# A graph network on one core: a second set of four selector buffers while adjacency matrices are built, and selectors made ahead of the adds

## The chip, the cores and the metric

The kernel runs on one core of a Trainium2 chip. The metric is the time of one execution on the device in microseconds; less is better. The core has five engines, each with an instruction queue of its own: TensorE (PE in the profile, its weight loads PEld), VectorE (DVE), ScalarE (ACT), GpSimd (POOL) and SyncE (SP). They order themselves by semaphores. TensorE reads SBUF and writes PSUM; a granted clock of 1.0 is 2.4 GHz, of 0.5 1.2 GHz.

## What is computed

Four blocks over one graph of 6250 nodes with 128 features and 106250 edges, sorted by destination: three layers of a relational convolution (8 relations, weights mixed of 4 bases), one weighted mean aggregation, two further relational layers, one unweighted mean aggregation. Each block ends in a residual and a layer norm. Cut to what matters:

```python
def rel_graph_conv(h, src, dst, etype, coef, bases, loopw, bias):
    c, hs = coef[etype], h[src]
    m = sum(c[:, b:b + 1] * (hs @ bases[b]) for b in range(4))
    return segment_sum(m, dst, num_segments=h.shape[0]) + h @ loopw + bias

def mean_layer(x, src, dst, weight, W, b):       # weight is 1 in the second one
    agg = segment_sum(x[src] * weight, dst, n)
    deg = clip(segment_sum(weight, dst, n), 1.0)
    return concatenate([x, agg / deg]) @ W.T + b

# block 1: x = layernorm(x + R(R(R(x)))), each R = relu(rel_graph_conv(h)) + h
# block 2: x = layernorm(x + mean_layer(x, edge_weight))
# block 3: x = layernorm(x + R5(R4(x)))           # relu(agg + x @ SW + b)
# block 4: x = layernorm(x + mean_layer(x, 1))
```

The kernel counts seven layers: 0, 1, 2 relational, 3 mean (weighted), 4, 5 relational, 6 mean.

## The kernel before

**A relational layer** runs over 832 tiles of 128 edges, 16 tiles a turn, 52 turns, in halves of 8 tiles (h = 0 and 1), each half in two quarters q of 4 tiles. GpSimd gathers the source rows of each tile by an indirect transfer into a ring of 16 slots (L630); it begins a half's 8 gathers when TensorE has summed that half of the turn before (`summed`). In every fourth turn slot 15 is filled by SyncE instead, which fetches 128 single rows (`lent`). VectorE makes one-hots over 16 destinations by 8 relations for each tile (`onehots`, L1284). TensorE multiplies rows by one-hots (the "sum", L1056, two PSUM banks), ScalarE moves the sums to SBUF (L763), TensorE multiplies them by the weights of the 8 relations (the "message", L1067, `MSG[h]`), and VectorE adds the 8 tiles' 16 columns to the accumulator one after the other (`adds`, L1296), because neighbouring tiles overlap.

The destinations come in 13 chunks of 512 nodes. When the turns that reach a chunk are over (about every four turns), each engine does a chunk step between two turns: `columns` (L1503, L1507) on VectorE, transposes on TensorE (L1104, L910), copies on ScalarE, in layers 2 and 5 the layer norm too.

**Filling.** The mean layers use a dense adjacency matrix, 6272 by 6272, in device memory. It is built from the edge list while the relational layers run: the weighted one in layers 1 and 2, the other one, of marks in bf16, in layers 4 and 5. Each half turn makes four "fills" of two windows each. For a fill f, VectorE makes selectors in SBUF (`hots`: L1377 the low selector, 2 x 196 columns, and L1381 twice the weighted row selector, or L1386 once the row marks); TensorE multiplies the two (`fill`, L946, bank AGG); ScalarE copies the bank to a staging buffer (`keep_fill`, L733) and after every second fill stores it (L737). Layer 0 builds nothing.

**The order around the change.** TensorE in a half: sum of quarter 0, fill 0, sum of quarter 1, fill 1, four relations' messages, fill 2, the other four, fill 3. The fill waits for `hots_made` and for `fill_kept`, and everything behind it in the queue waits with it. VectorE in a turn i: selectors of half 0, one-hots of half 1, adds of half 0, selectors of half 1, one-hots of half 0 of turn i+1, adds of half 1. There are four pairs of buffers, one for each f. The selectors for fill f wait until the fill f of the half before is done, since `filled` starts at 4:

```python
for f in range(4):
    dve.wait_ge(filled, H * 4 + (f + 1))
```

The adds of half h wait for `messaged[h]`, TensorE's last message of that half. So in the queue of VectorE the selectors of a half stand behind the adds of the half in front.

`rel_w` (8192 bytes in each of 128 partitions) holds the weights of layers 4 and 5. It is loaded by ScalarE's queue near the start (L686). The region `scratch` holds the selector buffers and the staging buffers. SyncE's `lend_passes` fetches the single rows and, in layer 0, lays the edge table from which the matrices' lists are gathered (`table_part`).

`P` is the number of passes over the edges, `more` is P - 1; with this graph P is 1 and `more` 0, and `more_slices` is 0 too: the branches for them are passed by.

## Time and profile before

| | us |
|---|---|
| median of 3 runs | 7132.64 (7103.35 to 7148.3) |
| the profiled execution | 7121.17 |
| its span, first to last instruction | 7118.9 |
| PE busy | 5280.1 (74%) |
| DVE busy | 3967.8 (56%) |
| POOL busy | 3900.0 (55%) |
| ACT busy | 1620.4 (23%) |
| mean granted TensorE clock | 0.808 |

Busy shares are means over stages with different limits, so the stages are read one by one. A row of the timeline names start, duration, engine, line, operation, the tensors out<-in, how often, and in brackets the idle time of the engine before it and what ended it. "issue" is idle time in which the engine waited for nothing that the profile shows. The selector buffers, the gathered rows and the sums all lie in one tensor called `bulk`. A matmul of f32 operands shows as two instructions.

### The profile page before, as it was taken

The numbers are of one execution on the slowest core, as the hardware profiler recorded it, in microseconds if no ns is written. First come the engines' busy times: TensorE is split into PE (matmuls) and PEld (weight loads), VectorE is DVE, ScalarE is ACT, GpSimd is POOL, SyncE is SP. The second block draws the span as 40 slices with busy tenths as digits, with TensorE's granted clock in tenths as the row PEclk, the third lists the DMA queues.
The fourth block names the chain that finished last, engine by engine and source line by source line (L and its number), as shares of the span: only waits on it lengthen the run. The fifth ranks groups of instructions, "written<-read, shape, count | busy, mean of one in ns | idle before, by whom it ended". The sixth has DMA issues, their size and how long they took to land.

```text
span 7118.9 us, 132757 instructions
## 1 busy us (share of the span) xinstructions
PE 5280.1 (74%) x25722; PEld 4285.0 (60%) x25723; DVE 3967.8 (56%) x10739; ACT 1620.4 (23%) x3108; POOL 3900.0 (55%) x4125
## 2 busy tenths in 40 slices
PE   6766667777777777777899866666676676667998
PEld 4655666666666666666555466665656666655554
DVE  3222226666666666666666555555545555556665
ACT  1111113322323222222100122222232222221000
POOL 6777776666666666666200066666656666662000
PEclk8777778988989889888899967767666666677998
DMA  3222224444444444444688544444434444445886
GB/s 97 63 67 67 70 69 115 125 124 121 128 123 115 120 114 123 117 117 116 198 285 279 192 118 121 123 120 125 121 110 117 114 119 114 113 117 192 277 284 201
DMA packets 719129, 966.83 MB, mean 136 GB/s; under 512 B 103155, under 2 KB 601199, under 8 KB 718543
## 3 DMA queue, kind: packets, MB, share of 16 engines
q0 software_dynamic: 131872, 271.19, 16.1%
q10 hardware_dynamic: 481717, 354.21, 15.9%
q1 hardware_dynamic: 105210, 338.21, 14.2%
q14 instruction: 267, 2.19, 0.1%
q8 instruction: 63, 1.03, 0.1%
HBM read 608.12 MB, written 361.06 MB: 136 GB/s over the span
## 4 chain that ended last, share of the span: by engine, by line
PE 52%; issue 15%; DVE 13%; POOL 9%; DVEq 6%; ACT 2%; DMA 1%; ACTq 0%; POOLq 0%; SPq 0%
PE msg L1067 17%; PE agg L946 10%; POOL bulk L630 9%; PE sum L1056 8%; DVE acc L1296 8%; PE sum L972 8%; PE msg L972 6%; DVEq L1296 2%; ACT bulk L763 2%; DVE bulk L1381 1%; DVE bulk L1386 1%; PE lin L920 1%; DMA bulk<-in_x_dram,srcT_i 1%; DVEq L159 1%; DVEq L1377 1%
## 5 line engine op out<-in xcount | busy, mean ns | idle before, releaser
L630 POOL DMA_INDIRECT bulk<-h_table,srcT_i x3276 | 3107.7, 949 | 2272.3 <-issue 927.8
L946 PE MATMUL agg<-bulk 128*128 128x196 f32 (+1 forms) x4992 | 1228.2, 364 | 1129.4 <-DVE bulk L1386 572.0
L1296 DVE TENSOR_TENSOR acc<-msg,acc 128x16 f32 x4160 | 728.9, 175 | 2307.5 <-PE msg L1067 1811.4
L1056 PE MATMUL sum<-bulk 128*128 128x128 f32 x8320 | 1539.2, 337 | 345.4 <-DMA bulk<-in_x_dram,srcT_i 210.0
L1056 PEld LDWEIGHTS sum<-bulk 128*128 128x128 f32 x8320 | 1383.2, 244 | 463.9 <-issue 251.2
L946 PEld LDWEIGHTS agg<-bulk 128*128 128x128 f32 (+1 forms) x4992 | 812.7, 188 | 1243.5 <-issue 1201.6
L733 ACT ACTIVATE bulk<-agg 128x392 f32<-128x392 f32 x1664 | 826.5, 497 | 2462.1 <-PE agg L946 2411.2
L1377 DVE TENSOR_TENSOR bulk<-iota_ps,low_key 128x392 f32<-128x392 f32 (+1 forms) x1664 | 927.9, 558 | 277.1 <-issue 277.1
L763 ACT ACTIVATE bulk<-sum 128x512 f32<-128x512 f32 x1040 | 621.1, 597 | 1680.3 <-PE sum L1056 1602.7
L630 POOL DMA_INDIRECT bulk<-in_x_dram,srcT_i x819 | 777.5, 949 | 279.5 <-issue 257.8
L1067 PE MATMUL msg<-bulk,mix_w 128*128 128x128 f32 x4992 | 834.3, 326 | 112.2 <-ACT bulk L763 101.2
L1067 PE MATMUL msg<-bulk,rel_w 128*128 128x128 f32 x3328 | 808.5, 422 | 123.4 <-ACT bulk L763 123.4
L1067 PEld LDWEIGHTS msg<-bulk,mix_w 128*128 128x128 f32 x4992 | 775.5, 236 | 185.3 <-issue 176.8
L1067 PEld LDWEIGHTS msg<-bulk,rel_w 128*128 128x128 f32 x3328 | 728.7, 322 | 196.6 <-issue 193.7
L1411 DVE TENSOR_TENSOR bulk<-bulk 128x1792 f32<-128x1792 f32 (+1 forms) x384 | 688.2, 1792 | 223.3 <-DMA bulk<-adjacency_w 97.4
L1284 DVE TENSOR_TENSOR bulk<-iota_ps,keyT 128x512 f32<-128x512 f32 x1040 | 665.0, 680 | 59.9 <-issue 45.0
L972 PE MATMUL sum<-bulk,hT 128*128 128x448 f32 x1568 | 660.8, 552 | 30.9 <-issue 13.4
L1381 DVE TENSOR_SCALAR bulk<-iota_ps,row_key,weight_of 128x128 f32<-128x128 f32 x1664 | 598.2, 400 | 0.0
L972 PEld LDWEIGHTS sum<-bulk,hT 128*128 128x128 f32 x1568 | 299.4, 194 | 329.1 <-issue 328.8
L972 PE MATMUL msg<-bulk,hT 128*128 128x448 f32 x1176 | 494.9, 544 | 0.0
L972 PEld LDWEIGHTS msg<-bulk,hT 128*128 128x128 f32 x1176 | 225.8, 192 | 222.1 <-issue 222.1
L1386 DVE TENSOR_TENSOR bulk<-iota_ps,row_key 128x256 bf16<-128x256 f32 x832 | 344.5, 414 | 0.0
(170 smaller groups left out, 1014.9 us busy)
## 6 DMA issues: line engine op xcount, KB each, us to landing
adjacency_w<-bulk ACTq DMA_DIRECT2D x416, 392.0 KB
adjacency_n<-bulk ACTq DMA_DIRECT2D x416, 392.0 KB
bulk<-adjacency_w SPq DMA_DIRECT2D x147, 896.0 KB, 4.6
bulk<-adjacency_n SPq DMA_DIRECT2D x147, 896.0 KB, 5.0
lent<-h_table SPq DMA_DIRECT2D x6656, 0.5 KB
bulk<-h_table,srcT_i POOLq DMA_INDIRECT x3276
lent<-in_x_dram SPq DMA_DIRECT2D x1664, 0.5 KB
bulk<-adjacency_w SPq DMA_DIRECT2D x49, 448.0 KB, 4.2
```

Source lines behind the costliest of these rows:

```text
L630: nc.gpsimd.indirect_dma_start(out=rows_in[:, s, :], out_offset=None, in_=rows_of[:, :], in_offset=bass.IndirectOffsetOnAxis(ap=srcT_i[:, ...
L733: act.activation(staged[s][:, f % 2 * 2 * LOWS:(f % 2 + 1) * 2 * LOWS], AGG[:, 0:2 * LOWS], ACT.Copy).then_inc(fill_kept, 1)
L763: act.activation(sums[:, h, :, 4 * (q % 2):4 * (q % 2) + 4, :].rearrange("p r t v -> p t r v"), SUM[q % 2][:, :].rearrange("p (t r v) -> p ...
L946: last = nc.tensor.matmul(AGG[:, w * LOWS:(w + 1) * LOWS], row[:, w, :], of[:, w, :], start=True, stop=True)
L972: last = nc.tensor.matmul(DENSE[s][:, 0:PIECE], x_rows[:, n, :], a_in[t % A_BUFS][:, s * PIECE:(s + 1) * PIECE], start=(n == 0), stop=(n = ...
L1056: last = nc.tensor.matmul(SUM[q % 2][:, t * KEYS:(t + 1) * KEYS], rows_in[:, 4 * q + t, :], onehot[:, 4 * q + t, :], start=True, stop=True)
L1067: last = nc.tensor.matmul(MSG[h][:, 0:HALF * WIN], W[:, n, :], sums[:, h, n, :, :].rearrange("p t v -> p (t v)"), start=(n == 0), stop=(n ...
L1284: nc.vector.tensor_tensor(onehot[:, 4 * q:4 * q + 4, :], IOTA[:, 0:KEYS].unsqueeze(1).broadcast_to(each), keyT[:, bass.ds(i * RING + 4 * q ...
L1296: nc.vector.tensor_tensor(acc[:, at], MSG[h][:, s * WIN:(s + 1) * WIN], acc[:, at], ALU.add).then_inc(added, 1)
L1377: nc.vector.tensor_tensor(low_hots[f] if weighted else low_marks[f], IOTA[:, KEYS:NATURAL].unsqueeze(1).broadcast_to(each), low_key[:, bas ...
L1381: ins = nc.vector.tensor_scalar(row_hots[f][:, n, :], IOTA[:, NATURAL:NATURAL + D], row_key[:, bass.ds(w + n, 1)], weight_of[:, bass.ds(w ...
L1411: nc.vector.tensor_tensor(a_sum[:, 0:wide], a_in[t % A_BUFS][:, 0:wide], a_sum[:, 0:wide], ALU.add).then_inc(a_counted, 1)
```

## The change

- VectorE's order in a building turn i is now: one-hots of half 1, selectors of half 1, adds of half 0, one-hots of half 0 of turn i+1, selectors of that half, adds of half 1. The selectors of the layer's very first half are made ahead of the loop.
- There are eight pairs of buffers: four for half 0, four for half 1. The second four low selectors and one row selector lie in `rel_w`'s memory, three row selectors behind the staging buffers in `scratch`. For the marks (bf16), which need half the bytes, the second set lies in the other half of the first four buffers and `rel_w` isn't touched.
- `filled` starts at 8 instead of 4, and the selectors for fill f wait for the fill f of two halves ago.
- `rel_w` is loaded at the head of layer 3 instead of near the start; TensorE waits for it in layers 4 and 5.
- The table of edges is laid in the last pass of layer 0 alone, where it was laid in every pass; with P = 1 that is the same work. A call outside of the loop takes the place of the loop's one round.

The diff, cut to its core:

```diff
-        low_hots = [scratch[:, f * 2 * LOWS:(f + 1) * 2 * LOWS].rearrange("p (w n) -> p w n", w=2) for f in range(4)]
-        row_hots = [scratch[:, 8 * LOWS + f * 2 * D:8 * LOWS + (f + 1) * 2 * D].rearrange("p (w n) -> p w n", w=2) for f in range(4)]
+        rel_w = sb("rel_w", [D, 2, N_RELS, D])
+        spare = rel_w[:, :, :, :].rearrange("p n r d -> p (n r d)")
+        kept_from = 8 * LOWS + 8 * D + 8 * LOWS
...
+        low_hots = pairs(scratch, 0, LOWS, 4) + pairs(spare, 0, LOWS, 4)
+        row_hots = pairs(scratch, 8 * LOWS, D, 4) + pairs(spare, 8 * LOWS, D, 1) + pairs(scratch, kept_from, D, 3)
...
-                with sp.Fori(0, P) as p:
+                def lend_pass(p, laying):
                     K = sp.snap(P * (REL_BEFORE[l] * QUADS) + p * QUADS)
                     for n in range(QUADS):
                         fetch(l, n, sp.snap(K + n))
                         place(n, sp.snap(K + n))
-                        if l == 0:
+                        if laying:
                             table_part(n)
...
+                with sp.If(more > 0):
+                    with sp.Fori(0, more) as p:
+                        lend_pass(p, False)
+                lend_pass(more, True)
...
-            act.dma_start(rel_w[:, :, :, :], rel_ws).then_inc(late_weights_in, 16)
...
-                act.wait_ge(filled, H * 4 + (f + 5))
+                act.wait_ge(filled, H * 4 + (f + 9))
...
                     if m == 0:
+                        act.dma_start(rel_w[:, :, :, :], rel_ws).then_inc(late_weights_in, 16)
...
-            pe.sem_inc(filled, 4)
+            pe.sem_inc(filled, 8)
...
                 for w in range(2):
-                    row, of = (row_hots[f], low_hots[f]) if weighted else (row_marks[f], low_marks[f])
+                    b = h * 4 + f
+                    row, of = (row_hots[b], low_hots[b]) if weighted else (row_marks[b], low_marks[b])
...
                         W = rel_w[:, layer["lin"] - 3, :, :]
+                        pe.wait_ge(late_weights_in, 48)
...
                     for f in range(4):
-                        dve.wait_ge(filled, H * 4 + (f + 1))
+                        dve.wait_ge(filled, H * 4 + (f + (5 if h is None else 1)))
...
                     def opened(p):
 
                         onehots(0, 0, dve.snap(count(P, p, r, 0)))
+                        if layer["fills"] and p is more:
+                            fill_at(0, 0)
                         dve.wait_ge(acc_set, 2 + CHUNKS * (r + 1))
 
                     def turn(i, k, filling=False):
-                        if filling:
-                            fill_at(i, 0)
                         onehots(1, i, k)
-                        adds(0, i, k)
                         if filling:
                             fill_at(i, 1)
+                        adds(0, i, k)
                         with dve.If(i < TURNS - 1):
-                            onehots(0, nc.s_assert_within(i + 1, min_val=1, max_val=TURNS - 1,
-                                                          skip_runtime_bounds_check_because="the condition above"), k + 1)
+                            following = nc.s_assert_within(i + 1, min_val=1, max_val=TURNS - 1,
+                                                           skip_runtime_bounds_check_because="the condition above")
+                            onehots(0, following, k + 1)
+                            if filling:
+                                fill_at(following, 0)
                         adds(1, i, k)
```

## Rows read from the trace of the kernel before

**Rows 1.** Busy time by stage: stretch, length, engines' busy (instructions), clock, DMA share, GB/s
```profile
core 0: us, PE busy (x) PEld busy (x) DVE busy (x) ACT busy (x) POOL busy (x), PEclk, DMA share, GB/s
200.00:1060.00 860.00, 594.67 (x2880) 514.66 (x2881) 243.51 (x894) 115.58 (x195) 650.45 (x685) 0.73 0.26 68
1086.00:2234.00 1148.00, 826.74 (x4994) 763.14 (x4993) 747.57 (x2269) 345.00 (x651) 777.12 (x819) 0.89 0.45 122
2262.00:3435.00 1173.00, 848.38 (x4999) 778.47 (x4997) 773.61 (x2407) 344.65 (x652) 775.61 (x818) 0.87 0.43 117
3460.00:4081.00 621.00, 589.61 (x1776) 311.43 (x1774) 403.99 (x427) 40.96 (x99) 0.00 (x0) 0.97 0.77 260
4083.00:5241.00 1158.00, 788.63 (x4157) 701.66 (x4155) 607.85 (x1848) 334.45 (x647) 774.64 (x819) 0.71 0.43 121
5271.00:6464.00 1193.00, 819.19 (x4184) 728.79 (x4182) 634.63 (x1972) 333.36 (x653) 776.05 (x818) 0.68 0.41 115
```

**Rows 2.** Waits, whole span: who waited for whom, us in total, times, longest
```profile
POOL bulk L630 <- PE sum L1056: 663.0, 306, 14.1
PE agg L946 <- DVE bulk L1386: 572.0, 208, 5.2
PE agg L946 <- DVE bulk L1381: 557.1, 207, 5.6
PE sum L1056 <- DMA bulk<-in_x_dram,srcT_i: 210.0, 313, 1.8
```

**Rows 3.** Timeline of TensorE in layer 1, one half turn
```profile
2025.54 0.90 PE L946 MATMUL agg<-bulk 128*128 128x196 f32 x4 [2.68 <-DVE bulk L1381]
...
2035.66 0.90 PE L946 MATMUL agg<-bulk 128*128 128x196 f32 x4 [2.77 <-DVE bulk L1381]
```

**Rows 4.** Timeline of VectorE in layer 1, the same stretch
```profile
2024.05 0.57 DVE L1377 TENSOR_TENSOR bulk<-iota_ps,low_key 128x392 f32<-128x392 f32 x1 [0.18 <-issue]
2024.53 0.72 DVE L1381 TENSOR_SCALAR bulk<-iota_ps,row_key,weight_of 128x128 f32<-128x128 f32 x2
...
2028.50 1.28 DVE L1284 TENSOR_TENSOR bulk<-iota_ps,keyT 128x512 f32<-128x512 f32 x2
2031.18 2.34 DVE L1296 TENSOR_TENSOR acc<-msg,acc 128x16 f32 x8 [1.41 <-PE msg L1067]
2034.16 0.57 DVE L1377 TENSOR_TENSOR bulk<-iota_ps,low_key 128x392 f32<-128x392 f32 x1 [0.64 <-issue]
```

**Rows 5.** Timeline of GpSimd in layer 1, the same stretch
```profile
2018.41 0.95 POOL L630 DMA_INDIRECT bulk<-h_table,srcT_i  x1 [2.02 <-PE sum L1056]
...
2024.67 0.95 POOL L630 DMA_INDIRECT bulk<-h_table,srcT_i  x1 [0.31 <-issue]
```

**Rows 6.** Timeline around a chunk step in layer 2, VectorE and TensorE
```profile
2857.27 0.60 PE L1104 MATMUL lin<-ident,y 128*128 128x128 f32 x4
2859.71 0.69 DVE L1503 SCALAR_TENSOR_TENSOR y<-acc,hT 128x512 f32 x1 [0.49 <-DVE acc L1296]
2863.04 2.07 PE L1056 MATMUL sum<-bulk 128*128 128x128 f32 x8 [4.21 <-issue]
2865.09 0.57 DVE L1377 TENSOR_TENSOR bulk<-iota_ps,low_key 128x392 f32<-128x392 f32 x1 [1.05 <-issue]
```

**Rows 7.** Timeline of TensorE in layer 4, a half at the lower clock
```profile
4605.74 1.11 PE L1056 MATMUL sum<-bulk 128*128 128x128 f32 x8
...
4614.73 1.94 PE L1056 MATMUL sum<-bulk 128*128 128x128 f32 x8
...
4621.75 1.08 PE L1056 MATMUL sum<-bulk 128*128 128x128 f32 x8
```

**Rows 8.** Timeline in layer 0: a gather and the sum that reads it
```profile
861.61 0.95 POOL L630 DMA_INDIRECT bulk<-in_x_dram,srcT_i  x1 [0.30 <-issue]
...
864.30 0.79 PE L1056 MATMUL sum<-bulk 128*128 128x128 f32 x2 [0.83 <-DMA bulk<-in_x_dram,srcT_i]
```

**Rows 9.** Timeline at the end of layer 1: last fill, next layer's first gather
```profile
2252.40 0.90 PE L946 MATMUL agg<-bulk 128*128 128x196 f32 x4
...
2262.00 0.95 POOL L630 DMA_INDIRECT bulk<-h_table,srcT_i  x1 [27.14 <-DMA h_table<-rows]
```

More of the change, by code:

```diff
@@ L244, in build, with pairs @@
         landed_i = scratch.bitcast(I32).rearrange("p (g t e) -> p g t e", t=3, e=D)
-        low_hots = [scratch[:, f * 2 * LOWS:(f + 1) * 2 * LOWS].rearrange("p (w n) -> p w n", w=2) for f in range(4)]
-        row_hots = [scratch[:, 8 * LOWS + f * 2 * D:8 * LOWS + (f + 1) * 2 * D].rearrange("p (w n) -> p w n", w=2) for f in range(4)]
-        low_marks, row_marks = ([hot.rearrange("p w n -> p (w n)").bitcast(BF16)[:, 0:2 * n].rearrange("p (w n) -> p w n", w=2) for hot in hots]
+        rel_w = sb("rel_w", [D, 2, N_RELS, D])
+        spare = rel_w[:, :, :, :].rearrange("p n r d -> p (n r d)")
+        kept_from = 8 * LOWS + 8 * D + 8 * LOWS
+        def pairs(at, first, n, many):
+            return [at[:, first + f * 2 * n:first + (f + 1) * 2 * n].rearrange("p (w n) -> p w n", w=2) for f in range(many)]
+        low_hots = pairs(scratch, 0, LOWS, 4) + pairs(spare, 0, LOWS, 4)
+        row_hots = pairs(scratch, 8 * LOWS, D, 4) + pairs(spare, 8 * LOWS, D, 1) + pairs(scratch, kept_from, D, 3)
+        low_marks, row_marks = ([hots[f].rearrange("p w n -> p (w n)").bitcast(BF16)[:, h * 2 * n:(h + 1) * 2 * n]
+                                 .rearrange("p (w n) -> p w n", w=2) for h in range(2) for f in range(4)]
                                 for hots, n in ((low_hots, LOWS), (row_hots, D)))
@@ L305, in build @@
         basis = sb("basis", [D, 3, N_BASES, D])
-        rel_w = sb("rel_w", [D, 2, N_RELS, D])
         mix_w = sb("mix_w", [D, N_RELS, D])
@@ L500, in lend_passes @@
                         place(n, sp.snap(K + n))
-                        if l == 0:
+                        if laying:
                             table_part(n)
+                if l:
+                    with sp.Fori(0, P) as p:
+                        lend_pass(p, False)
+                    return
+                more = sp.value_load(passes[0:1, 1:2], min_val=0, max_val=MAX_PASSES - 1)
+                with sp.If(more > 0):
+                    with sp.Fori(0, more) as p:
+                        lend_pass(p, False)
+                lend_pass(more, True)
             def load_adjacency(matrix, B, pass_of):
@@ L589, in gather_again @@
                     apart(pool)
-                pool.wait_ge(filled, pool.snap(built * FILLS + 4))
+                pool.wait_ge(filled, pool.snap(built * FILLS + 8))
                 apart(pool)
@@ L641, in _ @@
                     pool.wait_ge(at_set, 1)
-                    pool.wait_ge(edges_out, pool.snap(P * (16 * (3 * QUADS - WEIGHTS_FROM)) + 32))
-                    apart(pool)
+                    pool.wait_ge(edges_out, 16 * (3 * QUADS - WEIGHTS_FROM) + 32)
                     gather_lists()
@@ L936, in turn_lists, with fill @@
                 apart(pe)
-            def fill(H, f, weighted):
+            def fill(H, f, weighted, h=0):
                 pe.wait_ge(hots_made, H * 4 + (f + 1))
@@ L1038, in between @@
                         def between(h, f):
-                            fill(first + h, f, m == 0)
+                            fill(first + h, f, m == 0, h)
                         messages(i, k, between)
@@ L1262, in _ @@
                 if l == 1:
-                    dve.wait_ge(late_weights_in, 48)
+                    dve.wait_ge(late_weights_in, 32)
                     for n in range(2):
@@ L1368, in key_lists, with hots @@
                                             window_key[:, :].unsqueeze(2).broadcast_to([D, LANES, D]), ALU.subtract).then_inc(keys_ready, 1)
-                def hots(H, at, weighted):
+                def hots(H, at, weighted, h=None):
                     for f in range(4):
-                        dve.wait_ge(filled, H * 4 + (f + 1))
+                        dve.wait_ge(filled, H * 4 + (f + (5 if h is None else 1)))
                         apart(dve)
-                        w = at * 8 + 2 * f
+                        w, f = at * 8 + 2 * f, (h or 0) * 4 + f
                         each = [D, 2, LOWS]
@@ L1438, in fill_at @@
                         at = dve.snap(i * 2 + (part_of * 2 * TURNS + h))
-                        hots(dve.snap(at + (more_slices + 1) * HALVES) if of else at, at, of == 0)
+                        hots(dve.snap(at + (more_slices + 1) * HALVES) if of else at, at, of == 0, h)
                     def opened(p):
                         onehots(0, 0, dve.snap(count(P, p, r, 0)))
+                        if layer["fills"] and p is more:
+                            fill_at(0, 0)
                         dve.wait_ge(acc_set, 2 + CHUNKS * (r + 1))
                     def turn(i, k, filling=False):
-                        if filling:
-                            fill_at(i, 0)
                         onehots(1, i, k)
-                        adds(0, i, k)
                         if filling:
                             fill_at(i, 1)
+                        adds(0, i, k)
                         with dve.If(i < TURNS - 1):
-                            onehots(0, nc.s_assert_within(i + 1, min_val=1, max_val=TURNS - 1,
-                                                          skip_runtime_bounds_check_because="the condition above"), k + 1)
+                            following = nc.s_assert_within(i + 1, min_val=1, max_val=TURNS - 1,
[3 more added lines that the diff above has]
+                                fill_at(following, 0)
                         adds(1, i, k)
```

## The prediction, made before the change was run

> **What bounds the kernel now.** I read the busy times by stage first, with one stretch for each relational layer from its first gather to its last [rows 1]. Layer 0, which builds no matrix, issued 685 gathers in 860 us, 1.256 us for each; at that pace the 819 gathers of a layer take 1028 us. Layers 1, 2, 4 and 5, which build, took 1148, 1173, 1158 and 1193 us. They exceed the gathers' pace by 120, 145, 130 and 165 us, 560 us together. Everything the change can give lies in these four stretches and at their ends.
>
> The waits over the whole span come next [rows 2]: TensorE stood 557.1 us for the weighted selectors of layers 1 and 2 and 572.0 us for the marks of layers 4 and 5, each time at `fill`. GpSimd in its turn stood 663.0 us for a `sum` of TensorE, so it is not its own pace that holds it there. The wait for a gather, 210.0 us, belongs to layer 0 alone.
>
> The third view is one half turn on each engine. TensorE [rows 3]: the fill at 2025.54 and the fill at 2035.66 are the first ones of two halves, 10.12 us apart, and 2.77 us of this is idle until VectorE has made a selector. TensorE's own work in the half is 7.35 us. VectorE [rows 4]: selectors from 2024.05, one-hots from 2028.50, then 1.41 us idle until the messages of the half are there, the adds at 2031.18, and only behind them, at 2034.16, the selectors of the next half. This is the loop: messages, adds, selectors, fill, messages. The selectors cannot be made ahead, because they stand behind the adds in the queue and because their four buffers are those that TensorE is just reading. GpSimd [rows 5]: a gather is 0.95 us and the issue before it 0.30, but the first of a half waited 2.02 us for the sum that frees its slots. The loop sets the pace and GpSimd follows.
>
> **The change, part by part.** *Order and buffers.* The adds of a half now stand behind the selectors of the next one, which have buffers of their own. When TensorE reaches a fill, its selectors were made about one half earlier. The 557.1 + 572.0 = 1129 us of waiting leave TensorE. The gain is smaller, because another pace ends last then. Three candidates:
>
> GpSimd: 16, 16, 16 and 15 gathers in four turns are 15.75 a turn, by 1.256 us 19.8 us.
>
> VectorE: from the selectors at 2024.05 to those at 2034.16 are 10.11 us, less the wait of 1.41 us 8.70 us [rows 4]. This half has the 0.64 us of issue at the loop's end; with 0.18 in its place, as at 2024.05, the other half is 8.24 us, together 16.9 us. To this comes the chunk step: from 2859.71 to the selectors at 2865.09 are 5.4 us in layer 2 [rows 6], 12 or 13 times in 52 turns, 1.3 us a turn. About 18.2 us, 1.6 us under GpSimd. The marks are cheaper than the weighted selectors, so layers 4 and 5 have more room.
>
> TensorE: the layers' stretches less the waits at the fills are (1148 + 1173 - 557) / 104 = 17.0 us a turn for layers 1 and 2, and (1158 + 1193 - 572) / 104 = 17.1 for 4 and 5, chunk steps in it. That is 2.7 us under GpSimd. It holds for the clocks granted now, 0.89, 0.87, 0.71 and 0.68 [rows 1]. In layer 4 at 1.2 GHz (matmul groups of 1.94 us instead of 1.11) the stretch from one `sum` to that of the next half is 7.0 us [rows 7], with that one's own 1.94 us and a fill some 9.2, 18.4 us a turn and with the chunk steps (from 2857.27 to 2863.04, 5.8 us [rows 6], every fourth turn) 19.8: no more than GpSimd needs even if the higher level is never granted.
>
> So the four layers fall back on the gathers' pace, as layer 0 does. Bounds for what remains: none, or the whole of the present chunk steps' delay. In layer 2 such a step costs TensorE 4.21 us of idle and a first group at the lower clock, 2.07 us where 1.11 is usual [rows 6, 7], and 12 steps of 5 us are 60 us. Against that stands the room of the ring: with 16 slots, GpSimd gathers one half (10.0 us) while TensorE has the other to sum. A sum stands 2.7 us behind its gather in layer 0, from 861.61 to 864.30 [rows 8], so TensorE may be some 7 us late before GpSimd has to stand. One step fits, a step plus a slow half does not quite. I take 20 us a layer (1 us for each step, and a few for the first turn), 80 us together. Gain in the four stretches: 560 - 80 = 480 us.
>
> *The ends of the layers.* In layer 1 the last gather ended 27.14 us before the next layer's first one at 2262.00, at 2234.86, and the last fill started at 2252.40 [rows 9]: TensorE was still working through a backlog. At the gathers' pace there is none: 2.7 us from issue to sum and about 5 us for messages and fills, 8 us instead of 18. The tail behind it stays. 10 us by four layers are 40 us; bounds 0 and 44.
>
> *`rel_w` lends four buffers,* so its load of 1024 KB moves from the start to the head of layer 3 on ScalarE's queue. Nothing of ScalarE waits behind it but one issue. At the 260 GB/s that the DMA engines move in this stage [rows 1] it is 4 us of traffic in a stage in which TensorE is busy 589.61 of 621 us; between 0 and 4 us, I take 2. The wait for it in layer 4 stands 600 us later and costs nothing. At the start the traffic is saved; what is loaded there before the first gathers is not waited for, 0.
>
> *The rest* costs nothing: with one pass, SyncE's lending loop issues the same transfers behind one more branch, and it is ahead of TensorE; the table's rows are laid in the same places; the semaphore counts that start at 8 are the same instructions; the marks of the second set lie in the other half of the same floats. The selectors of the first half of a layer are made once ahead of the loop, 4.5 us of VectorE, in place of those in the first turn. The branch that now stands between the adds and the one-hots was covered by queued selectors before; if nothing covers it, it is a few tenths of a us a turn on VectorE, which has 1.6 to give.
>
> *A rule to weigh.* The gather that began at 2024.67 took its usual 0.95 us although VectorE's selectors filled the whole stretch around it, those with the scalar form from 2024.53 and again later [rows 4, 5]. So selectors and gathers pass each other without a price. The Trainium skill (SBUF — State Buffer, "Who interferes with whom") says that `tensor_scalar` can run in a mode that holds the port pair shared with GpSimd and blocks descriptor writing. By that rule this change, which packs VectorE tighter, would be paid in gathers; by the row it isn't, the trace disagrees with so broad a reading, and the page itself limits the mode to operands in SBUF, while the iota read here lies in PSUM.
>
> **Sum.** The profiled span of 7118.9 us - 480 - 40 + 2 = 6601 us. The run lasted 7121.17, 2 us more, and the median of the runs shown, 7132.64, lies 11 us above that: 6601 + 14 = 6615 us.
>
> **Rivals.**
> VectorE doesn't get ahead. It is one queue in order, and the adds still wait for messages. If it kept standing 1.41 us a half [rows 4], its turn would be 18.2 + 2.8 = 21.0 us, 52 turns 1092 us instead of 1048, four layers 176 us more: 6790 us. For it: 18.2 of 19.8 us leaves little, and after a chunk step it is late by about 4 us and wins back only 0.8 a half. Against it: TensorE is then waiting for gathers, so the wait at the adds is room and not loss. 0.13.
>
> TensorE's clock. Layer 0, which waits for gathers, was granted 0.73, layers 1 and 2 now 0.89 and 0.87 [rows 1]. If their level fell to 0.65, 17.0 us would be 17 x 0.88 / 0.65 = 23 us a turn, 1196 us a layer, nothing won in layers 1 and 2: 6615 + 2 x 148 = 6910 us. Against it: TensorE stands 24% of these layers now and would stand 14%. The Trainium skill (TensorE: Matmul & The Clock Gate, "Part 1: The HAM clock gate") has the lower level as the default that activity lifts; that speaks the same way. 0.06.
>
> The wait only moves. If TensorE stood at the fills as long as before, for instance because the selectors wait for buffers of `filled` counted wrongly late, nothing changes: 7130 us. Against it: the new count asks for the fill of two halves ago, which is behind the messages that the adds in front already waited for. 0.04.
>
> Slower. If GpSimd's gathers stood while VectorE runs the scalar-form selectors, eight pairs of 0.72 us a turn [rows 4] would be 5.8 us added to 19.8. Two weighted layers would lose 600 us against the 520 won: 7210 us or a little over. It decides from 5 us a turn on. The gather at 2024.67 is against it. 0.03.
>
> **How the numbers follow.** The forecast has 0.74, its own range 6550 to 6710 (no rest of the 80 us and 4 more at the ends below; twice the rest above). The range of 8 in 10 takes in the VectorE case: 6550 to 6800. A measurement of this kernel tells about 1% from no change. Faster by over 1%: forecast, VectorE and clock cases, 0.93. Within 1%: 0.04. Slower: 0.03.
>
> **What would show it.** The waits of TensorE for VectorE at `fill` gone (under 50 of 1129 us), waits for gathers in their place; the wait of GpSimd for `sum` under 80 us instead of 663.0; each of the four stretches within 1028 to 1065 us; the granted clock in layers 4 and 5 the same or higher; VectorE's wait for messages in the building layers still there and above 0.5 us a half; the fill after the last gather of layer 1 some 8 us behind it. The prediction is wrong if TensorE's time a turn without waits passes 19.8 us, if VectorE has no wait for messages left, or if the gathers' pace leaves 1.25 us.

## The result, and the profile after

The changed kernel takes 6482.93 us (median of four runs, 6481.08 to 6490.13), against 7140.47 us for the kernel before (four runs, 7103.35 to 7152.13). The ratio is 0.909 [0.906, 0.912]. The forecast of 6615 us had the direction and the mechanism, but the gain is larger than its range allowed: 6483 lies below the 6550 at which it began. The profiled execution took 6490.13 us with a span of 6488.0 us, 630.9 less than before; the forecast had taken 518 off the span.

The four layers that build, with the mean layer 3 between them, each from its first gather to its last. This is the table of busy times by stretch of the kernel after, with the granted clock (PEclk) and the share and rate of the DMA engines:

```profile
core 0: us, PE busy (x) PEld busy (x) DVE busy (x) ACT busy (x) POOL busy (x), PEclk, DMA share, GB/s
1083.60:2111.20 1027.60, 827.50 (x5021) 736.80 (x5020) 754.06 (x2292) 336.21 (x653) 775.52 (x819) 0.94 0.50 137
2128.60:3152.90 1024.30, 840.94 (x5017) 747.17 (x5016) 778.23 (x2433) 337.61 (x654) 774.84 (x819) 0.93 0.49 135
3184.00:3766.00 582.00, 574.74 (x1690) 300.48 (x1689) 382.17 (x355) 26.36 (x63) 0.00 (x0) 0.98 0.79 268
3794.70:4816.70 1022.00, 733.75 (x4184) 619.63 (x4183) 612.35 (x1862) 326.28 (x652) 772.51 (x818) 0.81 0.50 138
4833.40:5855.90 1022.50, 733.71 (x4204) 622.53 (x4202) 639.74 (x1994) 325.19 (x656) 773.12 (x818) 0.80 0.49 135
```

Set beside [rows 1], the stretches of layers 1, 2, 4 and 5 went from 1148, 1173, 1158 and 1193 us to 1027.6, 1024.3, 1022.0 and 1022.5. They are now all alike, and 819 gathers in 1022 us are 1.248 us each: the gathers' own pace and next to nothing beside it. TensorE's clock rose in all four, in layers 4 and 5 most, from 0.71 and 0.68 to 0.81 and 0.80.

The waits over the whole span (engine and line waited for, us in total, times, the longest):

```profile
DVE acc L1315 <- PE msg L1086: 1240.1, 394, 8.3
PE sum L1075 <- DMA bulk<-h_table,srcT_i: 642.2, 625, 3.1
POOL bulk L648 <- PE sum L1075: 53.7, 124, 12.5
```

The 557.1 and 572.0 us in which TensorE stood for VectorE at `fill` [rows 2] have no line left. At the sums of the building layers TensorE now waits for gathers, 642.2 us, where the kernel before has no such wait (its 210.0 us are those of layer 0, and 211.5 after). GpSimd's wait for a sum fell from 663.0 to 53.7 us, and 20.9 of these lie in layer 0. TensorE stands as much as the gathers leave it.

GpSimd, TensorE and VectorE in one turn of layer 1 (start, us, engine, line, tile; in brackets the idle time before and what ended it):

```profile
1995.10 0.94 POOL L648 DMA_INDIRECT bulk<-h_table,srcT_i  x1 [0.30 <-issue]
...
2005.08 0.94 POOL L648 DMA_INDIRECT bulk<-h_table,srcT_i  x1 [0.30 <-issue]
```

```profile
1997.61 0.48 PE L1075 MATMUL sum<-bulk 128*128 128x128 f32 x2 [1.96 <-DMA bulk<-h_table,srcT_i]
1997.98 1.26 PE L964 MATMUL agg<-rel_w,bulk 128*128 128x196 f32 x4
```

```profile
1995.08 1.29 DVE L1303 TENSOR_TENSOR bulk<-iota_ps,keyT 128x512 f32<-128x512 f32 x2
1996.29 0.56 DVE L1396 TENSOR_TENSOR bulk<-iota_ps,low_key 128x392 f32<-128x392 f32 x1
...
2003.26 2.33 DVE L1315 TENSOR_TENSOR acc<-msg,acc 128x16 f32 x8 [2.45 <-PE msg L1086]
...
2007.40 0.56 DVE L1396 TENSOR_TENSOR rel_w<-iota_ps,low_key 128x392 f32<-128x392 f32 x1
```

Before, a fill stood 2.77 us for a selector behind the adds [rows 3, 4]. Now selectors start at 1996.29 behind the one-hots, the adds of the half in front come at 2003.26, 2.45 us idle until their messages are there, and the fill at 1997.98 runs without waiting. The idle time is VectorE's. GpSimd's gathers follow each other every 1.25 us. And the views of GpSimd and TensorE show how much room the ring has. The fills around 1998 read `rel_w`, so the sum that ends at 1997.61 + 0.48 = 1998.09 is the last one of a half 1. Counted from the layer's first gather (16 a turn, 15 in every fourth), that is turn 45, the gather at 1995.10 opens half 0 of turn 46, and eight gathers later, at 2005.08, GpSimd asks for the slots of half 1 again. TensorE was 7.0 us ahead of that. The same difference for all halves of this layer, from the times at which the trace has the semaphore `summed` counted up, has a median of 7.6 us and never passes 8.2. Call this the margin; the experiments below act on it.

The end of layer 1, where [rows 9] showed a backlog: the last gather, the last fill and the next layer's first gather.

```profile
2111.19 0.94 POOL L648 DMA_INDIRECT bulk<-h_table,srcT_i  x1 [0.30 <-issue]
...
2128.55 1.03 POOL L648 DMA_INDIRECT bulk<-h_table,srcT_i  x1 [16.42 <-DMA h_table<-rows]
```

```profile
2118.94 0.90 PE L964 MATMUL agg<-rel_w,bulk 128*128 128x196 f32 x4
```

The last fill starts 6.8 us behind the last gather's end (2112.13) where it was 17.5, and GpSimd stands 16.42 us instead of 27.14.

### The profile page after: what moved, and what is told of

Read it like the earlier page. It is cut to its first block, busy times and chain, and to the rows that moved or that the text cites. A ratio compares the mean times of both kernels' runs of the same rounds, so it can differ in the third digit from the quotient of the medians.

```text
span 6488.0 us, 133021 instructions
## 1 busy us (share of the span) xinstructions
PE 5095.0 (79%) x25722; PEld 4005.7 (62%) x25723; DVE 3958.4 (61%) x10739; ACT 1581.1 (24%) x3108; POOL 3890.0 (60%) x4125
## 3 DMA queue, kind: packets, MB, share of 16 engines
q0 software_dynamic: 131872, 271.19, 18.2%
## 4 chain that ended last, share of the span: by engine, by line
POOL 49%; PE 22%; issue 22%; DMA 5%; DVE 1%; ACTq 1%; ACT 1%; POOLq 0%; DVEq 0%; SPq 0%
POOL bulk L648 49%; PE sum L990 8%; PE msg L990 7%; DMA bulk<-h_table,srcT_i 4%; PE sum L1075 2%; PE msg L1086 1%; PE agg L964 1%; DMA bulk<-in_x_dram,srcT_i 1%; PE iota_ps L1114 1%; PE lin L937 1%; PE lin L1115 0%; DMA bulk<-adjacency_w 0%; DMA bulk<-adjacency_n 0%; ACTq L688 0%; PE lin L1007 0%
## 5 line engine op out<-in xcount | busy, mean ns | idle before, releaser
L1075 PE MATMUL sum<-bulk 128*128 128x128 f32 x8320 | 1576.1, 318 | 1015.5 <-DMA bulk<-h_table,srcT_i 642.2
L1075 PEld LDWEIGHTS sum<-bulk 128*128 128x128 f32 x8320 | 1253.8, 212 | 1300.2 <-DMA bulk<-h_table,srcT_i 636.9
L1315 DVE TENSOR_TENSOR acc<-msg,acc 128x16 f32 x4160 | 728.2, 175 | 1746.8 <-PE msg L1086 1240.1
L1086 PE MATMUL msg<-bulk,mix_w 128*128 128x128 f32 x4992 | 856.4, 332 | 104.5 <-ACT bulk L779 90.7
L1086 PEld LDWEIGHTS msg<-bulk,mix_w 128*128 128x128 f32 x4992 | 796.8, 242 | 175.5 <-issue 168.0
L1086 PE MATMUL msg<-bulk,rel_w 128*128 128x128 f32 x3328 | 686.1, 372 | 120.8 <-ACT bulk L779 120.3
L964 PE MATMUL agg<-bulk 128*128 128x196 f32 (+1 forms) x3328 | 726.3, 326 | 20.6 <-ACT bulk L749 20.0
L1086 PEld LDWEIGHTS msg<-bulk,rel_w 128*128 128x128 f32 x3328 | 613.7, 276 | 179.5 <-issue 177.0
L1396 DVE TENSOR_TENSOR bulk<-iota_ps,low_key 128x392 bf16<-128x392 f32 (+1 forms) x1248 | 693.7, 556 | 0.0
L1400 DVE TENSOR_SCALAR bulk<-iota_ps,row_key,weight_of 128x128 f32<-128x128 f32 x1456 | 524.6, 402 | 0.0
L964 PEld LDWEIGHTS agg<-bulk 128*128 128x128 f32 (+1 forms) x3328 | 462.8, 161 | 67.7 <-issue 30.2
```

Of the source, the lines that this page charges most:

```text
L964: last = nc.tensor.matmul(AGG[:, w * LOWS:(w + 1) * LOWS], row[:, w, :], of[:, w, :], start=True, stop=True)
L1075: last = nc.tensor.matmul(SUM[q % 2][:, t * KEYS:(t + 1) * KEYS], rows_in[:, 4 * q + t, :], onehot[:, 4 * q + t, :], start=True, stop=True)
L1086: last = nc.tensor.matmul(MSG[h][:, 0:HALF * WIN], W[:, n, :], sums[:, h, n, :, :].rearrange("p t v -> p (t v)"), start=(n == 0), stop=(n ...
L1315: nc.vector.tensor_tensor(acc[:, at], MSG[h][:, s * WIN:(s + 1) * WIN], acc[:, at], ALU.add).then_inc(added, 1)
L1396: nc.vector.tensor_tensor(low_hots[f] if weighted else low_marks[f], IOTA[:, KEYS:NATURAL].unsqueeze(1).broadcast_to(each), low_key[:, bas ...
L1400: ins = nc.vector.tensor_scalar(row_hots[f][:, n, :], IOTA[:, NATURAL:NATURAL + D], row_key[:, bass.ds(w + n, 1)], weight_of[:, bass.ds(w ...
```

## Experiments

The theory going in: the order of VectorE's work, with buffers to allow it, broke the loop of messages, adds, selectors and fill; what binds now is the issue of the gathers; the chunk steps, to which the forecast gave 20 us a layer, are absorbed by the ring's margin.

### Which half of the change does it

*The buffers alone.* The changed kernel, with VectorE's loop put back:

```diff
                         onehots(0, 0, dve.snap(count(P, p, r, 0)))
-                        if layer["fills"] and p is more:
-                            fill_at(0, 0)
...
                     def turn(i, k, filling=False):
+                        if filling:
+                            fill_at(i, 0)
                         onehots(1, i, k)
+                        adds(0, i, k)
                         if filling:
                             fill_at(i, 1)
-                        adds(0, i, k)
                         with dve.If(i < TURNS - 1):
...
-                            onehots(0, following, k + 1)
-                            if filling:
-                                fill_at(following, 0)
...
                         adds(1, i, k)
```

> The changed kernel with VectorE's order put back: selectors of a half behind the adds of the half in front, but eight pairs of buffers. Theory (the order is what counts): the selectors stand behind the adds in the queue as before, so TensorE waits at the fills as before, about 1100 us in all, and the time is that of the kernel before, 7140 us within 1%. Rival (the buffers were what held VectorE back): 6480 to 6550 us.

Measured: 7125.06 us in ten runs (7108.92 to 7158.43), ratio 0.9992 [0.9979, 1.0006]. Its waits:

```profile
POOL bulk L648 <- PE sum L1075: 700.3, 314, 11.9
PE agg L964 <- DVE bulk L1405: 556.2, 208, 5.4
PE agg L964 <- DVE bulk L1400: 284.7, 103, 5.6
PE agg L964 <- DVE rel_w L1400: 269.6, 104, 3.0
```

The picture of [rows 2]: 556.2 for the marks, 284.7 + 269.6 = 554.3 for the weighted selectors in the two sets. Eight buffers alone give nothing, as its theory expected.

*The order alone.* The kernel before with four selector buffers, `rel_w` loaded at the start and the counts untouched; only VectorE's loop is the new one (the same lines, the other way round, and `fill_at(0, 0)` in `opened`).

> The kernel before with the new order of VectorE and nothing else: four pairs of buffers, the selectors for fill f wait for the fill f of the half in front, the weights of layers 4 and 5 are loaded at the start. Theory A (the order is enough): fills 0 to 2 free their buffers before the messages end, only the fourth pair of selectors (1.1 us) is made behind the last fill; VectorE keeps 8.7 us of work in the 10.0 us of a half, TensorE finds its first selectors ready, and the time is 6480 to 6530 us. Theory B (order and buffers are both needed): the adds now stand behind the fourth selectors, which wait for the last fill, and the loop of one half in front of the other closes again through TensorE; 6800 us or more.

Measured: 6487.7 us (6482.54 to 6498.28), ratio 0.9102 [0.9082, 0.9122], the whole gain. Its waits, and VectorE in a turn of layer 1:

```profile
DVE acc L1296 <- PE msg L1067: 579.6, 107, 8.9
DVE bulk L1377 <- PE agg L946: 566.0, 599, 2.2
POOL bulk L630 <- PE sum L1056: 52.2, 116, 13.4
```

```profile
2000.49 0.57 DVE L1377 TENSOR_TENSOR bulk<-iota_ps,low_key 128x392 f32<-128x392 f32 x1
2002.16 0.57 DVE L1377 TENSOR_TENSOR bulk<-iota_ps,low_key 128x392 f32<-128x392 f32 x1 [0.46 <-PE agg L946]
2003.37 2.32 DVE L1296 TENSOR_TENSOR acc<-msg,acc 128x16 f32 x8
2006.30 1.29 DVE L1284 TENSOR_TENSOR bulk<-iota_ps,keyT 128x512 f32<-128x512 f32 x2 [0.60 <-issue]
```

With four buffers VectorE has to wait for the fill that frees each one (566.0 us in 599 short waits). But when it comes to the adds their messages are there, for the messages come between the same fills: 566.0 + 579.6 = 1145.6 us, about the 1240.1 us that it stands at the adds with eight. The time is spent once, ahead of the selectors or behind them, and it was idle in either case. The prediction's sentence that the selectors can't be made ahead "because their four buffers are those that TensorE is just reading" was wrong as a bar: TensorE releases them one by one, early enough.

### What binds now

*One gather less.* A gather into slot 7 is left out in every turn of every relational layer, and slot 6 is read twice in its place:

```diff
-                                if s == RING - 1 and i % QUAD == QUAD - 1:
+                                if s == 7 or s == RING - 1 and i % QUAD == QUAD - 1:
...
+                                    slot = 6 if 4 * q + t == 7 else 4 * q + t
```

> The changed kernel without the gather of slot 7; TensorE reads slot 6 twice, so one tile of 16 has wrong rows, and the work of all other engines is the same. Theory (the gathers' issue on GpSimd sets the pace in all five relational layers): 52 gathers of 1.25 us less in each layer, 65 us a layer, 325 us in all, 6155 us. Rival (another engine is as near the bound): VectorE's estimated 18.2 us a turn in layers 1 and 2 against 18.4 us of the gathers' pace would just not show, but if its true need is 19 us or more, layers 1 and 2 give at most 35 us each and the time is 6215 us or more.

Measured: 6169.06 us (6168.78 to 6169.35), ratio 0.8651 [0.863, 0.8673]. Layers 1 and 4 of the stretches:

```profile
1020.80:1986.20 965.40, 795.93 (x5026) 718.48 (x5026) 748.84 (x2287) 334.81 (x653) 727.60 (x767) 0.95 0.50 142
3601.40:4558.60 957.20, 707.68 (x4191) 598.93 (x4190) 608.18 (x1861) 327.03 (x652) 723.66 (x767) 0.81 0.50 143
```

Of the 819 gathers 52 are gone, by 1.25 us 65 us; the stretches shrank by 62.2 and 64.8 us. Layer 0 loses its 52 gathers too; five such layers are the 314 us between 6482.9 and 6169.1, where 325 were expected. TensorE and VectorE execute what they did. So the gathers' issue alone binds in all four building layers, the heavier 1 and 2 as well.

### Why the chunk steps cost nothing

The forecast's residual of 80 us was for these steps. One in layer 2 after the change, on TensorE, with the next gather into the slots that its sums free:

```profile
2472.12 0.60 PE L1123 MATMUL lin<-ident,y 128*128 128x128 f32 x4
...
2477.61 2.07 PE L1075 MATMUL sum<-bulk 128*128 128x128 f32 x8 [3.93 <-issue]
...
2480.78 1.91 PE L1075 MATMUL sum<-bulk 128*128 128x128 f32 x8
```

```profile
2484.50 0.95 POOL L648 DMA_INDIRECT bulk<-h_table,srcT_i  x1 [0.30 <-issue]
```

The step is as long as in [rows 6]: 3.93 us idle, then a group of 2.07 us where 1.15 is usual. The half's last sum ends at 2480.78 + 1.91 = 2482.69, the gather starts at 2484.50. Of a margin of some 7 us 1.81 are left, and the gather doesn't wait. GpSimd's waits for a sum inside the stretches of layers 1, 2, 4 and 5, in this order:

```profile
POOL bulk L648 <- PE sum L1075: 10.6, 26, 3.0
POOL bulk L648 <- PE sum L1075: 7.0, 23, 0.3
POOL bulk L648 <- PE sum L1075: 6.4, 21, 0.3
POOL bulk L648 <- PE sum L1075: 8.8, 29, 0.3
```

All but one of these are 0.3 us, which passes between any two gathers. The one of 3.0 us lies in the first turns of layer 1, where no step is yet. So late sums cost the gathers of the four layers 2.7 us together, and the steps nothing. To find where the margin ends, the steps were made longer: in the building layers their four transposes are repeated.

```diff
-                    for s in range(blocks_of(c)):
+                    for s in list(range(blocks_of(c))) * (5 if layer['fills'] else 1):
```

Five times:

> The changed kernel with the transposes of each chunk step in the layers that build done five times over on TensorE, 16 transposes more, 2.2 us at 2.4 GHz and up to twice that at 1.2 GHz. Theory (TensorE's lateness at a step is taken up by the ring of 16 slots, margin some 7 us, so the steps cost nothing within the turns): only the steps behind the last turn of a layer cost, about 3 us by four layers, 6495 us, and GpSimd's wait for sums grows by less than 30 us. Rival, the term of the prediction (a step costs a share of its length, and a longer one more): 48 steps by 2.2 us, 105 us more, 6590 us or above.

Measured: 6482.1 us (6480.41 to 6492.67), ratio 0.909 [0.9072, 0.9107], nothing lost. The same place:

```profile
2472.10 2.35 PE L1123 MATMUL lin<-ident,y 128*128 128x128 f32 x20
2478.07 1.15 PE L1075 MATMUL sum<-bulk 128*128 128x128 f32 x8 [3.19 <-issue]
2479.72 1.05 PE L1075 MATMUL sum<-bulk 128*128 128x128 f32 x8
```

This run didn't do what it was made for. The transposes take 1.75 us longer, but the idle time behind them shrank and the sums ran at the higher clock, 1.15 us instead of 2.07. The half's last sum ended at 2480.77, 8.67 us after the transposes began, where it was 10.57 us in the changed kernel: 1.9 us less. It is not this step alone. Of the eleven steps between the turns of layer 2, nine had the group behind the idle time at 2.07 us before, and three have it in this run. GpSimd's wait for sums stayed at 51.6 us. It shows that these longer steps are free, but it puts no load on the margin.

Twenty-five times:

> The changed kernel with the transposes of each chunk step in the building layers done 25 times over: 96 transposes more, 13 us at 2.4 GHz, of which some 4 us can lie in the idle time that the step has anyway. Theory (the ring's margin, some 7 us, of which the usual step takes up to 5.6 us): now each step makes GpSimd wait, about 13 - 4 - 2 = 7 us or more of 48 steps, 340 us and up, plus some 60 us behind the last turns: 6800 to 7000 us, and GpSimd's wait for sums is over 300 us instead of 53.7. Rival (TensorE has so much room that steps of any such length vanish over the next turns): below 6600 us.

Measured: 6745.45 us (6731.59 to 6759.32), ratio 0.9452 [0.9381, 0.9524].

```profile
2520.04 11.08 PE L1123 MATMUL lin<-ident,y 128*128 128x128 f32 x100
...
2534.88 1.41 PE L1075 MATMUL sum<-bulk 128*128 128x128 f32 x8 [3.32 <-issue]
...
2537.38 1.85 PE L1075 MATMUL sum<-bulk 128*128 128x128 f32 x8
```

```profile
2540.04 0.94 POOL L648 DMA_INDIRECT bulk<-h_table,srcT_i  x1 [7.86 <-PE sum L1075]
```

```profile
POOL bulk L648 <- PE sum L1075: 247.8, 181, 12.8
```

Now GpSimd stands 7.86 us for the sum, and the gather comes 0.81 us after it ended (2537.38 + 1.85 = 2539.23). Ten us more on TensorE (11.08 instead of 0.60) cost 2.6, 6.0, 2.4 and 5.3 us a step in layers 1, 2, 4 and 5: their stretches are 1056.5, 1090.1, 1048.6 and 1081.0 us, 28.9, 65.8, 26.6 and 58.5 more, and the trace has eleven steps within each. That is 180 of the 241.5 us of span; the rest, 62 us, lies outside these stretches, where some 60 were expected. So the price is there, and it starts only when the margin is gone. Inside the stretches it was less than expected (180 us for 340, and 247.8 us of waiting where over 300 was expected). The kind was right; what was wrong was to take the step of layer 2 for all. In the changed kernel the margin behind a step has a median of 6.8 and 7.1 us in layers 1 and 4, by the same reckoning as above, and of 2.8 and 3.0 us in layers 2 and 5, where the step holds the layer norm: the layers whose steps leave little are those in which the longer step costs twice as much. Since 0.81 us pass between sum and gather even where GpSimd waits, of the 1.81 us in the unchanged step shown about 1.0 is true room, and that step has to be so much later before it costs anything.

### Is the second set worth anything once gathers bind less

The guess: eight buffers pay where VectorE is the bound. With three gathers left out in every turn (slots 3, 7 and 11; slots 2, 6 and 10 are read twice) the gathers' pace is 12.75 × 1.249 = 15.9 us a turn, under what VectorE takes.

> The changed kernel without the gathers of slots 3, 7 and 11, TensorE reading the slots in front twice: three tiles of 16 have wrong rows, all other work is the same. The gathers' pace is 12.75 x 1.25 = 15.9 us a turn. Theory (next to the gathers stands VectorE with 18.2 us a turn in the weighted layers 1 and 2, and TensorE and VectorE with 16 to 17 us in layers 4 and 5): layer 0 falls by 195 us, layers 1 and 2 by 75 to 90 us each, layers 4 and 5 by 140 to 180 us each, and GpSimd waits for sums in layers 1 and 2. Rival (the gathers bound everything still): 975 us less, 5510 us.

Eight buffers, measured: 5749.16 us (5745.55 to 5752.77), ratio 0.8056 [0.8008, 0.8104]. The same with the order alone and four buffers:

> The kernel of e2_order_only (new order, four pairs of buffers) without the gathers of slots 3, 7 and 11; three tiles of 16 have wrong rows as in e6_three_gathers_less. There, with eight pairs, layers 1 and 2 took 897 and 921 us and VectorE hardly waited; 5749 us. Theory (the second set counts where VectorE is the bound): with four pairs VectorE's fourth selectors wait for TensorE's last fill, so the two engines take turns in part; layers 1 and 2 take 940 us or more each, layers 4 and 5 870 or more, and the time is 5850 us or above. Rival (the second set is worth nothing here either): within 20 us of 5749 us.

That run was on another chip, where it took 8090.36 us and the kernel before 9199.64: ratio 0.8793 [0.8767, 0.8818], and nothing can be said of the pair. So the two were run again side by side.

> The kernel of e7_three_less_four_buffers (new order, four pairs of buffers, gathers of slots 3, 7 and 11 left out) again, next to its twin with eight pairs on the same chip, because in e7 the kernel before took 9200 us where it took 7140 us elsewhere, so that e7 and e6 can't be compared. Theory (the second set counts where VectorE is the bound): at least 100 us above the twin. Rival: within 20 us of it.

> The kernel of e6_three_gathers_less (new order, eight pairs of buffers, gathers of slots 3, 7 and 11 left out) again, as the twin of e8_four_buffers_again: 5749 us if the kernel before takes 7140 us on this chip, and at least 100 us less than the twin by the theory, the same within 20 us by the rival.

Again a chip of that kind: 7989.29 us with four, 7895.69 with eight, and 8996.09 for the kernel before; ratios 0.8881 [0.8855, 0.8906] and 0.8777 [0.8751, 0.8802]. There, with three gathers fewer, the second set is worth 94 us (two runs of each), but in another regime. The wait rows of the run with eight, and one copy of ScalarE beside its fill on TensorE:

```profile
POOL bulk L648 <- PE sum L1076: 2116.4, 378, 15.4
ACT bulk L749 <- remote: 1977.8, 373, 8.0
```

```profile
1610.07 0.90 PE L964 MATMUL agg<-rel_w,bulk 128*128 128x196 f32 x4
```

```profile
1614.11 0.50 ACT L749 ACTIVATE bulk<-agg 128x392 f32<-128x392 f32 x1 [4.18 <-remote]
```

The fill is over at 1610.97, and ScalarE goes on to its copy 3.1 us later, by a releaser that the view can't name. The trace has the semaphore `filled`, for which the copy waits, counted up at 1614.00, 3.0 us behind the fill's end; in the same kernel on the chip with 7140 us this is 0.01 us. The other thing that the copy waits for, the store that frees its staging buffer, can't be it: it had landed by 1608.01. GpSimd waits 2116.4 us for sums. So in this trace a signal between engines comes late; why is open. The change itself, with all its gathers, wasn't run on such a chip. All four were then run on one chip, with the kernel before at 7140.66 us.

> The changed kernel itself, as the twin of e11_order_only_again. On a chip on which the kernel before takes 7140 us: 6483 us, the same as the twin within 10 us. On a chip of the kind with 9000 us: the theory (there engines wake late from waits and the gathers do not bind any more) expects the twin with four pairs of buffers 50 to 150 us slower.

> The kernel of e2_order_only again (new order, four pairs of buffers, all gathers). 6488 us, the same as e10_changed_again, where the gathers bind; 50 to 150 us above e10 on a chip of the kind with 9000 us.

> The kernel of e8_four_buffers_again (new order, four pairs of buffers, gathers of slots 3, 7 and 11 left out) on this chip. By the theory (the second set counts where VectorE is the bound) 100 us or more above its twin e13, by the rival within 20 us.

> The kernel of e6_three_gathers_less (new order, eight pairs of buffers, gathers of slots 3, 7 and 11 left out) on this chip: 5749 us where the kernel before takes 7140 us; by the theory 100 us or more under its twin e12.

| kernel | four buffers | eight buffers |
|---|---|---|
| all gathers | 6490.73 (6487.83 to 6493.63), 0.9089 [0.9062, 0.9115] | 6494.05 (6487.75 to 6500.35), 0.9093 [0.9067, 0.912] |
| three fewer a turn | 5757.64 (5754.56 to 5760.73), 0.8062 [0.8039, 0.8085] | 5747.95 (5745.44 to 5750.46), 0.8048 [0.8025, 0.8072] |

The guess fell, on this kind of chip. Layers 1 and 4 with four buffers, then layers 1, 2 and 4 with eight:

```profile
939.30:1838.10 898.80, 749.74 (x4985) 671.03 (x4986) 736.02 (x2261) 339.27 (x646) 628.23 (x663) 0.98 0.53 144
...
3434.10:4263.90 829.80, 626.87 (x4167) 533.40 (x4165) 608.36 (x1853) 327.45 (x650) 624.87 (x663) 0.89 0.57 157
```

```profile
931.90:1830.30 898.40, 748.33 (x4985) 669.00 (x4986) 735.82 (x2261) 340.03 (x646) 630.39 (x663) 0.98 0.53 144
1855.10:2774.60 919.50, 776.53 (x4999) 691.72 (x4997) 764.98 (x2407) 341.88 (x652) 627.26 (x663) 0.96 0.51 139
3418.30:4250.30 832.00, 630.06 (x4172) 540.35 (x4171) 604.07 (x1856) 327.50 (x651) 626.84 (x663) 0.88 0.57 156
```

Layer 4 is still at its gathers' pace (663 × 1.25 = 829 us). Layers 1 and 2 are not; 898.4 and 919.5 us are 17.3 and 17.7 us a turn, and with eight buffers VectorE has no wait for messages in layer 1. There it is VectorE's own turn that is seen, and it has the same length with four buffers (898.8). In layer 1 with four, TensorE's waits at the fills and VectorE's for a buffer:

```profile
PE agg L946 <- DVE bulk L1382: 63.1, 84, 0.8
DVE bulk L1378 <- PE agg L946: 0.7, 2, 0.5
```

TensorE stands for selectors, and VectorE stands 0.7 us in all for a buffer: four are released as fast as VectorE fills them. With three gathers fewer the two kernels differ by 10 us, with two runs of each, their ratios' intervals overlap, and the 100 us that were looked for are not there. Layers 1 and 2 fell by 129 and 105 us, where 75 to 90 were expected for e6: VectorE needs less for a turn than the 18.2 us of the prediction.

## Why the prediction was right, and where it was short

- *What bounds, and what would.* Right. The stretches exceeded the gathers' pace by all that the loop cost and fell back on that pace. The run with one gather less confirms it.
- *The turns of the engines.* GpSimd 19.8 us: measured 1022 to 1028 us over 52 turns, 19.7. VectorE 18.2: 17.3 and 17.7 in the runs where it binds, so the estimate was 0.5 to 0.9 us high, and the room under GpSimd is 2 us or more rather than 1.6.
- *The residual of 20 us a layer* is the step that failed, and it carries most of the miss. The text itself put about 7 us of ring room beside a step of 5 us, and the room was right: 7.0 us in the turn shown, 7.2 to 7.6 in the median of each layer. Then came "one step fits, a step plus a slow half does not quite", and each step was charged 1 us and each layer a few more. Here it went wrong. A step with its slow half does fit: no step in the four layers left less than 1.5 us, and late sums cost the gathers 2.7 us in all, ahead of the first step. 80 us forecast, 2.7 measured. The other bound, none, stood in the text and was the right one.
- *The gathers' pace.* 1.256 us came from a stretch of layer 0 divided by its gathers. From one gather to the next it is 1.253 us in the mean in the trace of before and 1.250 in that of after (the median gather 0.947 and 0.944 us); the rest are a few longer gathers and waits in that stretch. The four stretches come out at 1.248 to 1.255. By 819 gathers and four layers this is 16 us. With the residual it makes 96: the stretches gave 4672 - 4096.4 = 575.6 us, not 480.
- *The ends of the layers.* The span lost 630.9 - 575.6 = 55 us outside the four stretches, and not 40 - 2. From the start of the last gather to the end of the last add the four ends took 21.2, 25.3, 24.3 and 26.9 us before and 10.4, 13.4, 10.4 and 11.0 after, 52.4 us less together, 10.8 to 15.9 each where 10 was forecast (in layer 1 the last fill stands 6.8 us behind the last gather, 8 forecast). The upper bound of 44 was too tight.
- *`rel_w` in layer 3, 2 us.* Open. From the last add of layer 2 to the first gather of layer 4 it took 622.4 us before, 622.0, 626.3 and 626.8 in the runs with four buffers and the early load, and 621.9 to 630.1 in seven with the late one. The spread is wider than the term.
- *Sum.* 96 + 15 = 111 of the 113 us by which the span was missed, and the other 2 are the term for `rel_w`, which the 55 us contain if it is real. About 19 us more are chance between the profiled run and the median: the median of before lay 11.5 us above its profiled run, that of after 7.2 below its own.
- *The range.* The bounds in the sum's own working reach to 6615 - 80 - 4 = 6531, and 6550 was written. Even 6531 would not have held 6483; what was missing is a bound below for the pace and a wider one for the ends.
- *Rivals.* VectorE doesn't get ahead (6790): no. Its wait for messages stayed (109, 84, 235 and 222 us in layers 1, 2, 4 and 5) and is room, as the text said against it. Clock (6910): the other way, up in all four layers. The wait only moves (7130): gone instead. Slower through gathers that stand beside the scalar-form selectors (7210): no. In layer 1, with VectorE busy 754 of 1028 us, the median gather is still 0.944 us. The Trainium skill (SBUF — State Buffer, "Who interferes with whom") lets `tensor_scalar` take the shared port pair only when its operands meet the conditions of a two-port mode; that they must lie in SBUF stands not there, as the prediction has it, but on the page it refers to (VectorE: DVE Perf Modes, "Why PSUM operands drop a tier"). In that narrow form the trace agrees with it.
- *The signs that were named.* Waits at `fill` under 50 us: 0. GpSimd for `sum` under 80: 53.7. Stretches 1028 to 1065: 1022 to 1027.6, just under the lower edge, where the residual should have been. VectorE's wait over 0.5 us a half: 0.93 in layers 1 and 2, 2.2 in layers 4 and 5. Fill behind the last gather of layer 1 some 8 us: 6.8.

What the prediction did not see at all: the change is two changes, and the one of them that its title names first, the second set, isn't needed on the chips on which the kernel before takes 7140 us. It argued that order and buffers belong together and never priced the order with the buffers there were.

## What to carry to other kernels

When an engine waits for work that stands behind other work in a queue, price a new order with the buffers there are before adding any: a waiting queue that waits somewhere else may cost nothing, and here it gave the whole 9%. When a slot ring feeds the bounding engine, measure its margin (from the end of the release to the next demand, in a normal turn and behind the longest step) and charge a late step only with what exceeds it. To read it off, count which gather opens a half: one gather astray is 1.25 us of margin. Take an issue pace from one instruction to the next, not from a stretch divided by its count.

## What the runs showed of the hardware

- An indirect gather of 128 rows costs GpSimd some 1.25 us (0.94 and 0.30 before it) in every layer, with VectorE busy 754 of 1028 us in layer 1 as with 612 of 1022 in layer 4, and with 68 GB/s on the DMA engines in layer 0 of the kernel before as with 135 to 138 in these stretches.
- More matmuls can leave TensorE earlier. With twenty transposes instead of four the group behind them took 1.15 us instead of 2.07 in the step shown, and from the start of the transposes to the half's last sum it took 1.9 us less; groups of 2.07 us fell from nine to three of the eleven steps of layer 2. The kernel's time stayed, because another engine binds. The Trainium skill (TensorE: Matmul & The Clock Gate, "Part 1: The HAM clock gate") has the lower level as the default that activity lifts; the two rows agree with it.
- Two chips took 9000 and 9200 us for the kernel before where three others took 7134 to 7143. In a trace from the one with 9000 us, engines go on several us after the work that they wait for is over (3.1 us in the copy shown), and the semaphore is counted up late. With three gathers fewer a turn, four buffers against eight differ by 94 us there, and by 10 here. A verdict on buffers holds for the chip on which it was taken.
